# Attention and mixture of experts on one core: weight splits, a table's steps, slots and gate powers moved in their engines' orders

## The chip, the cores and the metric

One core of one Trainium2 chip runs the whole program. The metric is the device time of one execution in microseconds (us). Of the kernel before there are three runs besides the profiled one.

## The reference

A pre-layernorm block on x of 4 x 1024 x 128 in float32, with two parts:

```python
x = x + attn(layernorm(x))         # scores = (h*w_lhs)(h*w_rhs)^T, softmax, times h; 4 sequences of 1024
x = x + ffn(layernorm(x))          # 4096 tokens, 8 experts, top 2
# ffn:
probs = softmax(xf @ router_w.T)
topk_probs, topk_idx = top_k(probs, 2); topk_probs /= topk_probs.sum(-1)
h   = gelu(xf @ w_fc[e] + b_fc[e])         # 128 -> 512
out = h @ w_proj[e] + b_proj[e]            # 512 -> 128
y   = sum over the two experts of gate * out
```

The output has the shape of x. The reference computes every expert for every token; the kernel computes only the two chosen ones.

## The kernel before, in words

Each of the five engines has one instruction stream, written out by hand; an engine does its instructions strictly in that order, and semaphores hold it where it needs another's result. So where a piece of work stands in an engine's stream decides what it can hold up.

**Attention.** The four sequences are batches b = 0 to 3. TensorE (PE) scores a batch in 16 blocks of 128 x 512, VectorE (DVE) takes row maxima (`row_max`, L1559), PE turns the negated maxima (`turn_negs`, L1211) and adds them to the scores, ScalarE (ACT) takes exponents, and PE multiplies them with the rows (`attend`, L1226). h and q are held as a high part (ACT, `high_parts`, L1002 and L1003) and a low part (DVE, `low_parts`, L1500 and L1507), because three products of short parts stand for one product in float32. Half a batch is a unit u, so `low_parts(2b+3)` is for the second half of the next batch; PE waits for it (`parts_made`) in the middle of the routing matmuls of the next batch (`route`, L1238 and L1239). `keep_hrw` (L1518) takes the routing products on DVE and `row_max(b+1, 1)` to `row_max(b+1, 7)` follow.

**Routing.** For each round of tokens (one batch, or half of batch 2) DVE picks the two experts (`picks`), PE counts ranks (`rank_round`, L1250 and L1256), DVE works out slots (`find_slots`, L1716 to L1739) and GpSimd (POOL) takes a power for the gates (`gate_powers`, L864), which `find_slots` waits for. A second layernorm goes with it: `take_stats2` (L1606), `take_moments2` (L1615), `scale_ln2` on POOL (its power is L817), `make_h2` and `high_h2` on ACT, `split_h2` on DVE (L1637).

**Dispatch.** POOL scatters each 128 tokens twice (for two experts) to their slots in memory: 16 indirect DMAs a batch (`dispatch`, L855). `dispatch_own`, `dispatch_max` and `dispatch_next` pace them by exponents and maxima. Batch 2's 16 stand after the batch loop, with `scale_ln2(6)`, `scale_ln2(7)` and `gate_powers(last)` among them. Batch 3's are done during the expert tiles.

**Weights.** w_fc is scaled and split in eight pieces of 512 columns: ACT makes the high part and scales the piece in place (`split_weights`, L1046 and L1047), POOL takes the difference (`low_part`, L825). When the first five are split, POOL clears their memory and stores empty rows from it (`clear_empty`, `store_empty`). PE waits for all eight before the first expert tile.

**Expert tiles.** 24 full tiles of 256 rows and 23 small ones of 128, in the order k = 0 to 46. Step k on PE turns tile k+2's rows (`turn_slots`, L1396), multiplies tile k up (`up`, L1409 to L1411) and tile k-2 down (`down`, L1430). Step 3 ends with a wait for tile 0's bias on DVE and `rank_round(last)`. DVE at step k adds the bias of tile k-3 (L1950), gates it (L1958) and keeps the row numbers of tile k (`keep_rows`, L1931 to L1943); between these it makes the tables that say which slots a tile takes: `second_table` is for tiles 8 to 15, a generator with one instruction a step (L485 to L623), stepped by `beside(k, n)` from the table `STEPS`. SyncE (SP) loads the tiles' slots (L737). Before tile 8 it waits until all scatters of batches 0 and 2 have landed and the second table is made (`more_dispatched(1)`).

## Time and profile before

| | |
|---|---|
| runs | 302.72, 300.7, 301.04 us; median 301.04 |
| profiled execution | 302.37 us, of which 300.6 us are the span of its instructions |
| busy, share of the span | PE 91%, PE weight load 82%, DVE 77%, ACT 65%, POOL 60% |
| mean granted clock of PE | 0.948 |
| chain that ended last | PE 66%, DVE 21%, DMA 5%, issue 4%, POOL 2% |
| first expert tile up | 153.3 us after the start |

Times in the rows are from the start of the span. The granted clock of PE has two levels here, 1.00 (2.4 GHz) and 0.50 (1.2 GHz). A busy share is an average over stages; what a change is worth is read from the stage that it touches. "Idle before" tells how long an engine had nothing to do and what ended that.

### The profile page before, as it was taken

To read this page: it belongs to the slowest core of one execution; us is meant where nothing else is said; L and a number is where in the kernel's file an instruction comes from. 1 tells how busy PE (TensorE), PEld (TensorE's weight loads), DVE (VectorE), ACT (ScalarE), POOL (GpSimd) and SP (SyncE) were. 2 spreads that over 40 slices of the span, in tenths; PEclk is the share of its full clock that TensorE was granted. 3 is DMA by queue.
4 is the path that set the end of the run, shared out by engine and by line. 5 is a ranking of instruction groups with operands and counts; after the bars stand their busy time and mean duration, and the time that the engine had idled before them with its cause. 6 is when DMAs were issued, how large, how long until landed. Compare 5 with 4: busy or idle time off the path is not lost.

```text
span 300.6 us, 8278 instructions
## 1 busy us (share of the span) xinstructions
PE 273.6 (91%) x2221; PEld 245.3 (82%) x2221; DVE 232.5 (77%) x1002; ACT 194.5 (65%) x425; POOL 181.3 (60%) x247
## 2 busy tenths in 40 slices
PE   7999999999999997999998699999999999999500
PEld 2689998888988987878888599999999999999400
DVE  5888899889878897998989668786565666763736
ACT  2437378896469590555679478677788878988300
POOL 8321036017677782687777657777777777777710
PEclk9989999999999996899999599999999999999955
DMA  5970000000401100011161034123433332212886
GB/s 193 410 312 0 0 3 0 3 0 0 146 27 57 45 19 20 28 47 36 60 165 52 29 100 138 56 74 100 115 88 99 99 99 83 83 56 68 346 283 258
DMA packets 15451, 28.52 MB, mean 95 GB/s; under 512 B 3904, under 2 KB 9920, under 8 KB 15152
## 3 DMA queue, kind: packets, MB, share of 16 engines
q1 hardware_dynamic: 10224, 16.88, 17.2%
q0 software_dynamic: 4608, 10.07, 10.0%
q10 hardware_dynamic: 576, 1.05, 1.0%
q8 instruction: 20, 0.33, 0.5%
q14 instruction: 23, 0.19, 0.2%
HBM read 15.83 MB, written 12.16 MB: 93 GB/s over the span
## 4 chain that ended last, share of the span: by engine, by line
PE 66%; DVE 21%; DMA 5%; issue 4%; POOL 2%; POOLq 0%; DVEq 0%; ACT 0%; SPq 0%
PE av_ps L1430 18%; PE av_ps L1226 15%; PE sc_ps L1409 5%; PE sc_ps L1411 4%; PE sc_ps L1410 4%; DVE neg_piece L1559 4%; PE bank L1396 2%; PE sc_ps L1215 2%; PE bank L1198 2%; PE sc_ps L1201 2%; PE sc_ps L1198 2%; PE sc_ps L1204 2%; PE bank L1204 2%; PE bank L1201 2%; DMA results<-prob,result_row 2%
## 5 line engine op out<-in xcount | busy, mean ns | idle before, releaser
L972 POOL DMA_INDIRECT results<-prob,result_row x71 | 69.7, 982 | 21.8 <-issue 14.9
L1121 ACT ACTIVATE raw_fc<-sc_ps,bfc,scale_down 128x128 f32<-128x128 f32 (+1 forms) x188 | 81.3, 530 | 2.1 <-PE sc_ps L1411 1.9
L855 POOL DMA_INDIRECT slots<-stage,slot x64 | 62.7, 980 | 24.5 <-issue 17.8
L1226 PE MATMUL av_ps<-h_all,prob 128*128 128x137 f32 x512 | 74.3, 289 | 2.6 <-DVE q_lo L1507 1.7
L1430 PE MATMUL av_ps<-raw_proj,raw_fc 128*128 x568 | 73.8, 281 | 0.7 <-DVE h_all L1950 0.7
L1226 PEld LDWEIGHTS av_ps<-h_all,prob 128*128 128x128 f32 x512 | 66.9, 192 | 7.5 <-DVE res L1587 2.8
L1430 PEld LDWEIGHTS av_ps<-raw_proj,raw_fc 128*128 128x128 f32 x568 | 68.3, 195 | 2.1 <-issue 1.6
L1409 PE MATMUL sc_ps<-h_all,wfc_hi 128*128 128x128 f16 (+1 forms) x188 | 43.7, 250 | 0.0
L1411 PE MATMUL sc_ps<-h_all,wfc_lo 128*128 128x128 f16 (+1 forms) x188 | 43.6, 250 | 0.0
L1410 PE MATMUL sc_ps<-h_all,wfc_hi 128*128 128x128 f16 (+1 forms) x188 | 43.6, 250 | 0.0
L1950 DVE TENSOR_TENSOR h_all<-av_ps,bpr 128x256 f32<-128x256 f32 (+1 forms) x47 | 16.9, 359 | 30.8 <-PE sc_ps L1411 27.1
L1113 ACT ACTIVATE h_all<-bank 128x512 f16<-128x512 f16 (+1 forms) x47 | 23.5, 501 | 24.8 <-PE sc_ps L1411 24.8
L1559 DVE TENSOR_REDUCE neg_piece<-bank 128x1 f32<-128x512 f32 x32 | 21.9, 685 | 6.2 <-PE sc_ps L1215 3.8
L1021 ACT ACTIVATE prob<-sc_ps 128x512 f32<-128x512 f32 x32 | 18.3, 598 | 9.8 <-PE sc_ps L1215 9.8
L1011 ACT ACTIVATE again<-bank 128x512 f32<-128x512 f32 x16 | 9.5, 595 | 21.1 <-DVE neg_piece L1559 21.1
L1559 DVE TENSOR_REDUCE neg_piece<-sc_ps 128x1 f32<-128x512 f32 x32 | 21.9, 683 | 1.2 <-PE sc_ps L1204 1.1
L1958 DVE TENSOR_SCALAR prob<-h_all,row_gate 128x128 f32<-128x128 f32 x71 | 19.7, 304 | 1.4
L1409 PEld LDWEIGHTS sc_ps<-h_all,wfc_hi 128*128 x188 | 18.5, 99 | 1.5 <-issue 0.2
L1411 PEld LDWEIGHTS sc_ps<-h_all,wfc_lo 128*128 x188 | 18.6, 99 | 1.3
L1410 PEld LDWEIGHTS sc_ps<-h_all,wfc_hi 128*128 x188 | 18.6, 99 | 1.0
L1396 PE MATMUL bank<-ident,slots_in 128*128 128x128 f16 x142 | 15.6, 222 | 0.1
L1198 PE MATMUL bank<-hT_hi,q_hi 128*128 128x512 f32 x32 | 14.8, 463 | 0.0
(208 smaller groups left out, 533.5 us busy)
## 6 DMA issues: line engine op xcount, KB each, us to landing
slots_in<-slots SPq DMA_DIRECT2D x24, 132.0 KB, 2.5
raw_fc<-in_w_fc_dram SPq DMA_DIRECT2D x1, 2048.0 KB, 11.2
raw_proj<-in_w_proj_dram SPq DMA_DIRECT2D x1, 2048.0 KB, 15.6
res<-in_x_dram SPq DMA_DIRECT2D x3, 512.0 KB, 5.7
slots_in<-slots SPq DMA_DIRECT2D x23, 66.0 KB, 2.2
results<-prob,result_row POOLq DMA_INDIRECT x71, 2.3
slots<-raw_fc POOLq DMA_DIRECT2D x2, 528.0 KB, 4.1
slots<-stage,slot POOLq DMA_INDIRECT x64, 2.4
```

The costliest lines, as they stand in the source:

```text
L855: pool.indirect_dma_start(out=slots[:, :], out_offset=bass.IndirectOffsetOnAxis(ap=slot[:, n, k:k + 1], axis=0), in_=stage[:, b % 2, t, :] ...
L972: pool.indirect_dma_start(out=results[:, :], out_offset=bass.IndirectOffsetOnAxis(ap=result_row[a][:, h:h + 1], axis=0), in_=gated[a][h], ...
L1113: act.activation(xT[:, a % NH, 0:n], bank[a % 2][:, :].bitcast(F16)[:, 0:n], ACT.Copy).then_inc(xT_made, 1)
L1121: ins = act.activation(hid[:, a % NH, c, 0:halves_of(k) * P], up_ps(k, c), ACT.Gelu_apprx_tanh, bias=bfc[:, e, c:c + 1], scale=scale_down[ ...
L1198: pe.matmul(o, q_hi[:, a, rows], hT_hi[:, a, cols], start=True, stop=False, skip_group_check=True)
L1226: mm = pe.matmul(att[:, t, 0:AUG], probT[:, m % RING, t * P:(t + 1) * P], h_aug[:, b % 2, exp_rows(n), :], start=(n % BT == 0 and t % 2 == ...
L1396: mm = pe.transpose(o[:, part * w + h * P:part * w + (h + 1) * P], x, ident16[:, :])
L1409: pe.matmul(o, wfc_hi[:, e, of], xT[:, a % NH, 0:w], start=True, stop=False, skip_group_check=True)
L1410: pe.matmul(o, wfc_hi[:, e, of], xT[:, a % NH, w:2 * w], start=False, stop=False, skip_group_check=True)
L1411: mm = pe.matmul(o, wfc_lo[:, e, of], xT[:, a % NH, 0:w], start=False, stop=True, skip_group_check=True)
L1430: mm = pe.matmul(o, hid[:, a % NH, c, rows], wpr[:, e, c, :], start=(c == 0 and h == 0), stop=(c == HC - 1), skip_group_check=True)
L1559: dve.tensor_reduce(neg_piece[:, r // TU, r % TU, c:c + 1], block_bank(n), AX_X, ALU.max, negate=True).then_inc(max_made, 1)
```

## The change

Six edits, all of order:

1. POOL: `low_part(5)`, `(6)`, `(7)` are made in batch 1 (5 before `clear_empty`, 6 after `store_empty`, 7 behind `scale_ln2(2)` and ahead of batch 0's scatters) instead of batch 2. In batch 2 all five `dispatch_own(1)` scatters come before `scale_ln2(4)`; two did before.
2. ACT: `split_weights(5)`, `(6)` in batch 1 behind `high_h2(1)` and before `high_parts(5)`, `(7)` at the start of batch 2, instead of between batch 2's exponents.
3. PE: two matmuls on constant data (`stay_busy(2)`) in batch 0 after the first five routing tiles.
4. DVE at the end of batch 1: `find_slots(0)` and `add_logits(2)` right behind the last `shift_again`, ahead of `low_parts(5)`; `split_h2(1)` and `take_stats2(2)` behind `keep_hrw(2)`.
5. DVE at the tiles: `second_table` is stepped at tiles 1 to 5 and inside `find_slots(last)`, not at tiles 1 and 2 alone.
6. POOL: `gate_powers(last)` is put ahead of scatter 12 of batch 2, not behind it.

```diff
--- before.py
+++ after.py
@@ -829,6 +829,7 @@
                 pool.wait_ge(inv_made, u + 1)
 
             EMPTY_PIECES = -(-E * H * ROW // HID)
+            assert EMPTY_PIECES + 3 == PIECES
 
             def clear_empty():
                 pool.wait_ge(w_split, EMPTY_PIECES)
@@ -923,16 +924,15 @@
                     gate_powers(ROUNDS_BY[b - 1] - 1)
                 if b == 1:
                     beside_sums(2 * b)
-                    for i in range(3, EMPTY_PIECES):
+                    for i in range(3, EMPTY_PIECES + 1):
                         low_part(i)
                     clear_empty()
                     for half in range(2):
                         store_empty(half)
+                    low_part(EMPTY_PIECES + 1)
                 if b == B - 2:
-                    beside_sums(2 * b)
-                    for i in range(EMPTY_PIECES, PIECES):
-                        low_part(i)
-                    dispatch_own(b - 1, 0)
+                    for part in range(2):
+                        dispatch_own(b - 1, part)
                 if b == 0:
                     pool.wait_ge(peak_made, 1)
                     pool.partition_all_reduce(peaks[:, :], peak[:, :], P, RMAX).then_inc(peaks_made, 1)
@@ -945,9 +945,9 @@
                 if b + 1 < B:
                     scale_ln2(2 * b)
                 if b == 1:
-                    dispatch_own(b - 1, 0)
-                if b >= 1 and b + 1 < B:
-                    dispatch_own(b - 1, 1)
+                    low_part(EMPTY_PIECES + 2)
+                    for part in range(2):
+                        dispatch_own(b - 1, part)
 
             for i in range(8):
                 dispatch(B - 2, i)
@@ -955,10 +955,9 @@
             for i in range(8, 11):
                 dispatch(B - 2, i)
             scale_ln2(2 * B - 1)
-            for i in range(11, 13):
-                dispatch(B - 2, i)
+            dispatch(B - 2, 11)
             gate_powers(len(ROUNDS) - 1)
-            for i in range(13, SCATTERS):
+            for i in range(12, SCATTERS):
                 dispatch(B - 2, i)
 
 
@@ -1057,6 +1056,8 @@
                 if b == 1:
                     split_weights(0)
                     split_weights(1)
+                if b == B - 2:
+                    split_weights(7)
                 keep_again(b, 0)
                 if b == 1:
                     split_weights(2)
@@ -1081,13 +1082,13 @@
                         normalise(2 * b + 2 + u, t + 1)
                     if n in (3, 5) and b == 1:
                         split_weights((n + 3) // 2)
-                    if n in (3, 5, 7) and b == B - 2:
-                        split_weights((n + 7) // 2)
                     if n >= BT - 2 and b >= 1 and b != B - 2:
                         for t in (0, 1) if n == BT - 2 else (2, 3):
                             make_h2(2 * b - 1, t)
                         if n == BT - 1:
                             high_h2(2 * b - 1)
+                            if b == 1:
+                                split_weights(5)
                 keep_rows(2 * b + 1)
                 for n in range(BT, EXPS):
                     if n in (BT + 2, BT + 3) and b == B - 2:
@@ -1097,6 +1098,8 @@
                             high_h2(2 * b - 1)
                     if n == BT + 1 and b + 1 < B:
                         high_parts(2 * b + 2)
+                    if n == BT + 5 and b == 1:
+                        split_weights(6)
                     if n == BT + 5 and b + 1 < B:
                         high_parts(2 * b + 3)
                     exponent(b, n)
@@ -1299,6 +1302,7 @@
                     attend(b - 1, 15)
                 if b == 0:
                     route(0, range(5))
+                    stay_busy(2)
                 pe.wait_ge(again_kept, TU * b + 3)
                 turn_negs(2 * b)
                 pe.wait_ge(again_kept, TU * b + 4)
@@ -1864,12 +1868,10 @@
                     find_slots(ROUNDS_BY[b - 1] - 1, measure)
                     steps(norm, 2)
                 if b + 1 < B:
-                    if b == 1:
-                        split_h2(2 * b - 1)
                     low_parts(2 * b + 2)
                     for r in (2, 3):
                         shift_again(b, r)
-                if b == B - 2:
+                if 1 <= b < B - 1:
                     find_slots(b - 1)
                     add_logits(2 * b)
                 if b == 0:
@@ -1878,20 +1880,18 @@
                     low_parts(2 * b + 3)
                 if b == 0:
                     find_scales()
-                if 1 <= b < B - 2:
-                    find_slots(b - 1)
                 if b + 1 < B:
 
-                    if b != B - 2:
+                    if b == 0:
                         add_logits(2 * b)
                     if b == B - 2:
                         early = picks(ROUNDS_BY[b] - 2)
                         steps(early, 6)
                     row_max(b + 1, 0)
-                    if b != B - 2:
+                    if b == 0:
                         take_stats2(2 * b)
                     keep_hrw(b + 1)
-                    if b == B - 2:
+                    if b >= 1:
                         take_stats2(2 * b)
                         split_h2(2 * b - 1)
                 if b == B - 1:
@@ -1910,7 +1910,7 @@
             choose = picks(last)
 
 
-            STEPS = {0: choose, 1: second_table, 2: second_table, 6: late_table, 7: late_table, 8: late_table, 9: late_table,
+            STEPS = {0: choose, 1: second_table, 2: second_table, 3: second_table, 4: second_table, 5: second_table, 6: late_table, 7: late_table, 8: late_table, 9: late_table,
                      10: small_table, 11: small_table, 12: small_table, 13: small_table}
 
             def beside(k, n=1):
@@ -1986,14 +1986,14 @@
                     add_bias(k - 3, (a - 3) % NB)
                     gate(k - 3, (a - 3) % NB)
                 if k == 4:
-                    find_slots(last)
+                    find_slots(last, lambda: beside(k))
                 for j in range(rows_by(k - 1), rows_by(k)):
                     keep_rows(j, j % NB)
                 if k >= 6:
                     add_bias(k - 3, (a - 3) % NB)
                     beside(k)
                     gate(k - 3, (a - 3) % NB)
-                beside(k, {0: 30, 1: 6, 2: 40, 6: 3, 7: 3, 8: 3, 9: 40, 13: 40}.get(k, 3))
+                beside(k, {0: 30, 1: 3, 2: 0, 3: 2, 4: 8, 5: 40, 6: 3, 7: 3, 8: 3, 9: 40, 13: 40}.get(k, 3))
                 if k == NTILES - 1:
                     add_results(0)
                 if k == 2:
```

## Rows read from the trace of the kernel before

**Rows 1.** Windows: length, busy time of PE, PEld, DVE, ACT, POOL, granted clock, DMA.

```profile
16.00:20.20 4.20, 3.74 (x28) 3.43 (x27) 3.92 (x17) 1.79 (x3) 0.56 (x2) 0.98 0.99 425
20.20:23.60 3.40, 3.40 (x9) 2.64 (x9) 2.66 (x14) 1.88 (x5) 2.27 (x5) 0.52 0.16 63
...
115.80:122.60 6.80, 6.80 (x23) 5.89 (x24) 4.96 (x21) 0.60 (x1) 2.11 (x3) 0.51 0.07 22
...
163.60:167.00 3.40, 1.00 (x9) 0.81 (x8) 3.12 (x23) 3.31 (x7) 1.29 (x2) 0.97 0.13 42
167.00:173.80 6.80, 5.96 (x38) 5.27 (x39) 4.67 (x24) 2.38 (x6) 4.80 (x4) 0.51 0.10 32
```

**Rows 2.** Timeline of DVE and POOL, end of batch 2: start, length, instruction, idle before.

```profile
109.01 3.16 DVE L1716 TENSOR_TENSOR pick<-pick,rank 128x64 f32<-128x64 f32 x2
...
108.56 3.38 POOL L825 TENSOR_TENSOR wfc_lo<-raw_fc,wfc_hi 128x512 f16<-128x512 f32 x3
```

**Rows 3.** Timeline of PE, the wait that follows in batch 3's routing.

```profile
115.16 0.47 PE L1226 MATMUL av_ps<-h_all,prob 128*128 128x137 f32 x2 [1.75 <-DVE q_lo L1507]
```

**Rows 4.** Timeline of PE at steps 3 (its rank round), 5 and 6 of the tiles.

```profile
167.84 0.25 PE L1250 MATMUL av_ps<-taken,before 128*128 128x80 f16 x1 [3.25 <-DVE h_all L1950]
...
174.14 0.39 PE L1396 MATMUL bank<-ident,slots_in 128*128 128x128 f16 x4
...
177.46 0.39 PE L1396 MATMUL bank<-ident,slots_in 128*128 128x128 f16 x4
```

**Rows 5.** Timeline of DVE at steps 1 to 3 of the tiles.

```profile
163.50 0.42 DVE L563 TENSOR_TENSOR chosen<-past,per_expert 128x256 f32<-128x256 f32 x1
...
164.30 0.16 DVE L569 TENSOR_SCALAR of_expert<-of_expert 128x8 f32<-128x8 f32 x1
...
166.95 0.16 DVE L1693 TENSOR_TENSOR step_down<-best 128x8 f32<-128x8 f32 x1
...
167.36 0.42 DVE L1950 TENSOR_TENSOR h_all<-av_ps,bpr 128x256 f32<-128x256 f32 x1
```

**Rows 6.** Timeline of POOL: scatters 12 and 15 of batch 2 and the gates' power.

```profile
164.21 0.98 POOL L855 DMA_INDIRECT slots<-stage,slot  x1 [0.30 <-issue]
167.40 1.67 POOL L864 TENSOR_TENSOR gate<-euler,gap 128x8 f32<-128x8 f32 x1 [2.20 <-DVE gap L1698]
...
172.04 0.96 POOL L855 DMA_INDIRECT slots<-stage,slot  x1 [0.30 <-issue]
```

**Rows 7.** Line L737, SP's loads of tiles: tile 8's issue, and the landings.

```profile
L737 SPq DMA_DIRECT2D slots_in<-slots x1: 333/333/333, 175.1 to 175.1; - x1
...
DMA to landing us min/median/max: 2.3/2.5/2.7
```

**Rows 8.** Timeline of ACT, its first work in batch 2.

```profile
82.33 0.60 ACT L1011 ACTIVATE again<-bank 128x512 f32<-128x512 f32 x1 [4.11 <-DVE neg_piece L1559]
```

**Rows 9.** Timelines of DVE and PE, the edge from batch 1 to 2.

```profile
78.04 0.35 DVE L1716 TENSOR_TENSOR pick<-pick,rank 128x64 f32<-128x64 f32 x2
...
81.62 0.68 DVE L1559 TENSOR_REDUCE neg_piece<-bank 128x1 f32<-128x512 f32 x1
...
80.39 0.25 PE L1239 MATMUL bank<-rw_parts,hT_lo 128*128 128x8 f32 x1
...
87.33 0.60 PE L1211 MATMUL bank<-ident,neg_cols 128*128 128x128 f32 x4
```

**Rows 10.** Timelines of DVE and PE, the edge from batch 2 to 3.

```profile
118.45 0.29 DVE L1518 TENSOR_REDUCE h_all<-bank 128x64 f32<-128x128 f32 x1 [1.68 <-PE bank L1239]
...
120.29 0.68 DVE L1559 TENSOR_REDUCE neg_piece<-bank 128x1 f32<-128x512 f32 x1
...
127.02 0.63 PE L1211 MATMUL bank<-ident,neg_cols 128*128 128x128 f32 x4
```

**Rows 11.** Timelines of POOL and DVE: a small POOL power beside a DVE instruction.

```profile
160.98 1.05 POOL L817 TENSOR_TENSOR rstd<-var,minus_half 128x4 f32<-128x4 f32 x1
...
161.15 0.22 DVE L1679 TENSOR_TENSOR pick<-pick,first_id 128x64 f32<-128x64 f32 x1
```

## The prediction

> **What bounds the kernel now.** I began with the page: PE is busy 91% of the span, so a gain must come from PE's idle time or its clock. PE's waits by line came next and hold only two that matter: 3.25 us at the tiles' rank round and 1.75 us in batch 3's routing. Then the granted clock by windows, because a short wait can cost more than itself. The reader is to see three stretches at half level, 20.2 to 23.6, 115.8 to 122.6 and 167.0 to 173.8; ahead of the third PE was busy 1.00 of 3.40 us [rows 1]. The last two follow the two waits.
>
> The first wait begins on POOL. Its three low parts run from 108.56 to 111.94, and two DVE picks started at 109.01 need 3.16 us [rows 2]. The second half's low q, behind them on DVE, holds PE from 113.41 to 115.16 [rows 3]. The second wait begins on DVE: the second table's steps stand ahead of tile 0's bias, so PE idles from 164.59 to 167.84 [rows 4, 5].
>
> A third limit has no wait yet. POOL's last scatter of batch 2 starts at 172.04 [rows 6], SP's load of tile 8 at 175.1, and a load lands after 2.3 to 2.7 us [rows 7]; PE turns that tile at 177.46 [rows 4]. It is just in time: PE cannot get to step 6 earlier than this chain allows.
>
> **The change part by part.**
>
> Splits on ACT (edit 2). The same six activations are moved. Piece 7 falls into the 4.11 us in which ACT waits at the start of batch 2 [rows 8]. Cost nothing, covered by idle time; if pieces 5 or 6 found none, each would put about 1.3 us before an exponent or high part. Batch 2's exponents lose three splits, but PE paced them; I take no gain.
>
> Low parts (edit 1). POOL has 3.38 us less at 108.56 and as much more earlier: 1.13 a piece. Pieces 5 and 6 delay only scales that are not due. Piece 7 stands ahead of batch 0's scatters, which run back to back, and with a later second-layernorm scale (below) they come about 1.75 us later (1.13 and some 0.6), and so does `gate_powers(1)`, from 108.56 [rows 2] to 110.3. The picks cost 0.35 where no low part runs [rows 9] against 3.16: DVE wins 2.8 us there, and the slots' chain then reaches its wait for the power only at about 110.9 (109.01, the edge's 0.9 below, 1.0 of slots), 0.5 us after it. The three `dispatch_own(1)` scatters put ahead of `scale_ln2(4)` go into time in which POOL waited; by batch 2's scatters about 0.6 us are left of this, and `scale_ln2` has its moments no earlier.
>
> Reorder on DVE (edit 4). `find_slots(0)` fills a DVE gap, but `take_stats2(2)` and `split_h2(1)` now stand between `keep_hrw(2)` and the second row maximum. Routing ends on PE at 80.64, so that maximum can start at 80.68 plus 1.84, the distance from L1518 to L1559 in the same order one batch later [rows 10], 82.52, against 81.62 [rows 9]. It sets `keep_again`, the scores behind it and `turn_negs(4)`: +0.9 us at 87.33. Between +1.0 and 0, if PE has slack that I don't see; I take +0.9, because the rows stand back to back.
>
> The edge to batch 3. PE comes to its wait at 113.41 + 0.9 = 114.31; low q, 2.8 us sooner but for the edge's 0.9 and some 0.3 of wait for ACT's high q, is ready at about 113.6 by PE's wake at 115.16. So the wait goes. PE went from 115.16 to `keep_hrw` at 118.45 [rows 3, 10], 2.65 us of it at half level; at full level that is about 1.97 us, so `keep_hrw` is at 116.3 and the maximum at 118.1. From there DVE is back to back in the rows: 127.02 - 120.29 = 6.73 us [rows 10], whatever PE's clock. `turn_negs(6)` comes at 124.85, so attention ends **2.15 us** earlier, the 0.9 included. Ends: 0.9 later (wait and half level stay) and 3.1 earlier (no edge cost).
>
> Two busy matmuls (edit 3). At half level nine matmuls take 3.40 us, 0.38 each [rows 1], so two take less than that each at full level, and PE is idle 0.46 us of 16.0 to 20.2. They cost 0 to 0.3 us. If they hold the clock, 3.40 us at half level shrink by half, 1.7; DVE then binds part of it, so **-1.6**. Ends 0.3 and -1.7. What speaks for it: only narrow routing products and that idle precede the fall.
>
> The tiles (edits 5 and 6), in times of before. In `keep_rows(2)` L563 starts at 163.50 as now; the way to L569 is 0.80 [rows 5]; one more step and the last two row instructions take about 0.53; then from L1693 to L1950 0.41 as now: tile 0's bias starts at 165.24, not 167.36, and the rank round at 165.72. PE's idle shrinks from 3.25 to 1.13 us. A full tile is 3.32 us (177.46 - 174.14) [rows 4]; rank round and step 4 took 6.30 us at half level, and take some 3.72 at full. So PE is at step 6 at 165.72 + 3.72 + 3.32 = 172.8. The second table's last steps fall into `find_slots(last)`, about 170.2, before anyone needs them; if that cover were gone, tile 8's load would wait for the table.
>
> But tile 8 isn't there. The power starts when the gap is made, at 165.28. From power to last scatter were 4.64 us (172.04 - 167.40) with three scatters behind it; edit 6 makes it four, and one is 0.96 + 0.30 = 1.26 [rows 6]. POOL is free at about 163.3 (0.30 before 164.21, and 0.6 sooner), so the moved scatter, which fitted before the power, is lost to waiting. Last scatter 171.18; load 3.06 later; turned 2.36 after that: 176.6 against 177.46, **-0.86** [rows 4, 6, 7]. PE idles 3.8 us. That is longer than the 3.25 us after which the level fell, so I expect half level again: **+2.6** (6.30 - 3.72), between 0 (level holds, or fell at the 1.13 us idle and ran out under the stall) and 3.4 (6.80 us wholly at half level [rows 1]).
>
> Sum: -2.15 - 1.6 - 0.86 + 2.6 = -2.0. The profiled execution takes 302.37 us, 1.33 above the median of the runs, 301.04; the forecast is 300.4 for the one and **299.0** for the other.
>
> **A rule weighed against a row.** POOL's scales of batch 1 move later by the two pieces, beside DVE instructions with two inputs from SBUF. In the trace a POOL power runs from 160.98 to 162.03 and a DVE instruction of that kind started in it at 161.15 takes 0.22 us [rows 11]: no hold. The Trainium skill (SBUF — State Buffer, Who interferes with whom) says that such a DVE instruction contends with a GpSimd instruction that reads SBUF, and that the later one is fully blocked. The three low parts agree with it, this small power does not; by the rule up to 1.05 us would come on top at batch 2's maxima and the sum would be -1.0, by the row it is -2.0. I take the row, the same operation and shape.
>
> **Rivals.**
> 1. The busy matmuls don't hold the clock: all else as forecast, 301.04 - 0.4 = 300.6. For: 0.45 us of work in 4.2 us is little. Against: routing mixed with `attend` keeps full level in other batches.
> 2. Tile 8's stall costs no clock: 301.04 - 4.6 = 296.4. For: PE may be at half level already and arrive later. Against: 1.13 us amid dense matmuls is less than any wait that a fall follows.
> 3. Slower: `low_part(7)` ahead of batch 0's scatters. If `gate_powers(1)` ends more than 1 us later than worked out (after 113), `find_slots(1)` waits for it, `low_parts(7)` with it, PE's wait and half level at 115 come back with the edge's 0.9, the busy matmuls save little, and the tiles cost 1.7: 0.9 + 1.7 and about 0.5 of added wait, 304.1. Against: 0.5 us margin on DVE and 0.7 on PE.
>
> **How the numbers follow.** Forecast 0.36, rival 1 0.22, rival 2 0.26, rival 3 0.16. About 1% (3.0 us) is what a measurement can tell from no change. Faster by more: rival 2 almost whole and the third of the forecast in which the half level is short, 0.35. Slower by more: half of rival 3 and a little beside, 0.10. Within: 0.55. The range goes from below rival 2 to inside rival 3, 295.8 to 303.3; the forecast's own, with the half level's price 0 to 3.4 reduced to 1.3 to 3.4, is 297.7 to 299.8.
>
> **What would show it.** Right: no half level before the tiles; DVE's L1716 of batch 2 under 0.5 us; PE's L1226 without its 1.75 us; rank round idle near 1.1 us; the gates' power starting right at DVE's gap with POOL idle before it; a PE wait of nearly 4 us at tile 8's turn, half level behind it. Wrong: a half level at 20 or 115; a power idle under 1 us, which makes edit 6 a gain; no stall at step 6, which would mean that the scatters came sooner than POOL's rows allow.

## The result, and the profile after

The changed kernel takes **297.6 us** (median of 4 runs, 297.55 to 297.99), the kernel before in the same comparison 301.11 (300.7 to 302.72). The ratio is 0.9875, with a 95% interval of 0.9839 to 0.9911: 3.5 us faster, where 299.0 was forecast. (The quotient of the two medians is 0.9883.) It is clearly faster than no change, and by its medians it is 1.2%, over the 1% that the prediction took as the least that a measurement can tell; but that 1% lies inside the interval. The forecast of 299.0 was a gain of 0.7%. The profiled execution took 297.55 us, so it stands for its median; that of the kernel before was 1.33 us above its own, so between the two profiled executions there are 4.8 us, not 3.5.

The page of the changed kernel: its span, its busy times, and PE's granted clock in 40 slices of 7.4 us. The last line is the granted clock of the kernel before, in 40 slices of its own span. Here and below, rows that the argument doesn't need are left out between those shown.

```profile
span 295.8 us, 8282 instructions
PE 269.2 (91%) x2223; PEld 240.1 (81%) x2223; DVE 229.1 (77%) x1002; ACT 194.9 (66%) x425; POOL 181.6 (61%) x247
PEclk9999999999999999999999979999999999999955
PEclk9989999999999996899999599999999999999955
```

The span is 4.8 us shorter, and PE is busy for as large a share of it as before. Apart from the last two slices, which are alike in both, only one slice is left below full level. The first three windows of [rows 1], one from the tiles' rank round to step 5, and two at the turn of tile 8 say which (us, then PE's busy time with the number of instructions, granted clock, DMA share, GB/s):

```profile
16.00:20.20 4.20, 4.20 (x30) 1.00 1.02 437
20.20:23.60 3.40, 3.40 (x21) 1.00 0.11 39
115.80:122.60 6.80, 5.97 (x32) 1.00 0.12 41
161.50:169.80 8.30, 7.44 (x73) 1.00 0.13 42
169.80:172.20 2.40, 0.00 (x0) 1.00 0.38 90
172.20:175.70 3.50, 3.46 (x19) 0.58 0.65 176
```

The two stretches at half level in attention are gone, and so is the one after the tiles' rank round. A new one begins at 172.2, behind 2.4 us in which PE did nothing. Of PE's waits by line (us in total, times, longest), these name the cause:

```profile
PE bank L1400 <- DMA slots_in<-slots: 2.4, 1, 2.4
...
PE av_ps L1253 <- DVE h_all L1950: 0.9, 1, 0.9
PE av_ps L1434 <- issue: 0.8, 1, 0.8
```

The 3.25 us at the rank round are 0.9 here, and the 1.75 us for the low q in batch 3's routing have no line any more. In their place PE waits 2.4 us for the rows of tile 8, and 0.8 us in step 4. The timeline of PE gives the checkpoints of attention: `turn_negs(1)`, the second turn of batch 0, and `turn_negs(4)` and `turn_negs(6)`, the first turns of batches 2 and 3 (start, us, engine, line, operation, out<-in):

```profile
33.36 0.60 PE L1214 MATMUL bank<-ident,neg_cols 128*128 128x128 f32 x4
86.57 0.60 PE L1214 MATMUL bank<-ident,neg_cols 128*128 128x128 f32 x4
123.06 0.63 PE L1214 MATMUL bank<-ident,neg_cols 128*128 128x128 f32 x4 [0.41 <-DVE neg_cols L1579]
```

Before, the second and third were at 87.33 and 127.02 [rows 9, 10]. On DVE, the edge from batch 1 to 2 and the picks of batch 2:

```profile
79.01 0.29 DVE L1522 TENSOR_REDUCE h_all<-bank 128x64 f32<-128x128 f32 x1 [1.71 <-PE bank L1242]
80.86 0.68 DVE L1563 TENSOR_REDUCE neg_piece<-bank 128x1 f32<-128x512 f32 x1
108.23 0.36 DVE L1720 TENSOR_TENSOR pick<-pick,rank 128x64 f32<-128x64 f32 x2
109.09 0.16 DVE L1730 TENSOR_SCALAR gate_sum<-gate 128x8 f32<-128x8 f32 x1
111.25 0.74 DVE L1511 SCALAR_TENSOR_TENSOR q_lo<-bank,w_d,q_hi 128x512 fp32r<-128x512 f32 x1
```

The two picks take 0.36 us, against 3.16 beside the low parts [rows 2]. The second half's low q is ready at 111.99; its user on PE, which stood at 115.16 [rows 3], now runs without a wait. POOL, first at `gate_powers(1)` in batch 2, then around the tiles' gates:

```profile
107.23 1.68 POOL L865 TENSOR_TENSOR gate<-euler,gap 128x8 f32<-128x8 f32 x1
158.47 1.08 POOL L856 DMA_INDIRECT slots<-stage,slot  x1 [0.47 <-issue]
161.12 1.67 POOL L865 TENSOR_TENSOR gate<-euler,gap 128x8 f32<-128x8 f32 x1 [1.58 <-DVE gap L1702]
166.88 0.96 POOL L856 DMA_INDIRECT slots<-stage,slot  x1 [0.30 <-issue]
```

`gate_powers(1)` ends at 108.91, 0.35 us later than before. POOL then stands idle 1.58 us ahead of the tiles' power, where a scatter fitted before, and the last scatter of batch 2 starts at 166.88. PE in the first tiles, the rank round, step 4 with its second product, and the turns of the tiles' rows in steps 5, 6 and 7:

```profile
161.57 0.21 PE L1253 MATMUL av_ps<-taken,before 128*128 128x80 f16 x1 [0.85 <-DVE h_all L1950]
164.41 2.05 PE L1434 MATMUL av_ps<-raw_proj,raw_fc 128*128 x16 [0.77 <-issue]
166.29 0.39 PE L1400 MATMUL bank<-ident,slots_in 128*128 128x128 f16 x4
172.22 0.40 PE L1400 MATMUL bank<-ident,slots_in 128*128 128x128 f16 x4 [2.44 <-DMA slots_in<-slots]
177.40 0.39 PE L1400 MATMUL bank<-ident,slots_in 128*128 128x128 f16 x4
```

And SP's queue, whose first load in this window is that of tile 8 (5 loads grouped):

```profile
169.95 5.32 SPq L737 DMA_DIRECT2D slots_in<-slots  x5
```

**Where the time went.** Attention ends 3.96 us sooner (127.02 to 123.06). The rank round comes 6.27 us sooner (167.84 to 161.57), tile 8 is turned 5.24 us sooner (177.46 to 172.22) [rows 4], and step 6 then takes 5.18 us instead of 3.3, because PE runs it at half level. Step 7 began at 180.81 before, so there 180.81 - 177.40 = 3.4 us are left. The remaining 1.4 us between the two spans arise at the very end. Before, DVE waited there for the load of the early results:

```profile
279.80 0.69 DVE L1965 TENSOR_TENSOR res<-res,hT_hi 128x512 f32<-128x512 f32 x1 [0.52 <-DMA hT_hi<-results]
```

Its two additions stood ahead of the last three biases, and PE's last product waited 0.72 us for DVE. In the changed kernel this load is issued 6.2 us sooner (269.97, was 276.13), DVE has no such wait, and the last gates end 4.2 us sooner (279.49, was 283.73). The other 0.6 us arise between these gates and the last addition. It is partly chance that the 3.4 us at step 7 equal the difference of the medians, since the profiled executions differ by 4.8.

### The profile page after: what moved, and what is told of

It is laid out like the page before. It is cut to its first block, busy times and chain, and to the rows that moved or that the text cites. A ratio compares the mean times of both kernels' runs of the same rounds, so it can differ in the third digit from the quotient of the medians.

```text
span 295.8 us, 8282 instructions
## 1 busy us (share of the span) xinstructions
PE 269.2 (91%) x2223; PEld 240.1 (81%) x2223; DVE 229.1 (77%) x1002; ACT 194.9 (66%) x425; POOL 181.6 (61%) x247
## 4 chain that ended last, share of the span: by engine, by line
PE 69%; issue 10%; POOL 9%; DMA 5%; DVE 5%; ACT 1%; SPq 0%; POOLq 0%; DVEq 0%; ACTq 0%
PE av_ps L1434 20%; PE av_ps L1229 15%; POOL slots L856 7%; PE sc_ps L1413 5%; PE sc_ps L1415 5%; PE sc_ps L1414 5%; PE bank L1400 2%; PE bank L1201 2%; PE sc_ps L1218 2%; PE bank L1204 2%; PE sc_ps L1204 2%; PE sc_ps L1207 2%; PE sc_ps L1201 2%; DMA raw_fc<-results 2%; PE bank L1207 2%
## 5 line engine op out<-in xcount | busy, mean ns | idle before, releaser
L971 POOL DMA_INDIRECT results<-prob,result_row x71 | 68.7, 967 | 23.9 <-issue 12.5
L856 POOL DMA_INDIRECT slots<-stage,slot x64 | 63.6, 994 | 24.7 <-issue 16.1
L1229 PE MATMUL av_ps<-h_all,prob 128*128 128x137 f32 x512 | 73.3, 286 | 0.7 <-DVE lg_part L1594 0.4
L1434 PE MATMUL av_ps<-raw_proj,raw_fc 128*128 x568 | 73.0, 279 | 0.8 <-issue 0.8
L1229 PEld LDWEIGHTS av_ps<-h_all,prob 128*128 128x128 f32 x512 | 66.1, 190 | 5.5 <-DVE res L1591 2.7
L1434 PEld LDWEIGHTS av_ps<-raw_proj,raw_fc 128*128 128x128 f32 x568 | 67.6, 193 | 2.2 <-issue 1.5
L1958 DVE TENSOR_SCALAR prob<-h_all,row_gate 128x128 f32<-128x128 f32 x71 | 20.6, 324 | 1.3
```

Source lines behind the costliest of these rows:

```text
L856: pool.indirect_dma_start(out=slots[:, :], out_offset=bass.IndirectOffsetOnAxis(ap=slot[:, n, k:k + 1], axis=0), in_=stage[:, b % 2, t, :] ...
L971: pool.indirect_dma_start(out=results[:, :], out_offset=bass.IndirectOffsetOnAxis(ap=result_row[a][:, h:h + 1], axis=0), in_=gated[a][h], ...
L1229: mm = pe.matmul(att[:, t, 0:AUG], probT[:, m % RING, t * P:(t + 1) * P], h_aug[:, b % 2, exp_rows(n), :], start=(n % BT == 0 and t % 2 == ...
L1434: mm = pe.matmul(o, hid[:, a % NH, c, rows], wpr[:, e, c, :], start=(c == 0 and h == 0), stop=(c == HC - 1), skip_group_check=True)
```

## The experiments

Each run is compared with the kernel before on the same chip. The runs were made in three groups on three chips; the kernel before had medians of 300.67 (e1 to e4), 301.37 (e5 to e8) and 301.2 (e9 to e12). In the second group e5 is the changed kernel itself, in the third e9 is the kernel of e6; e1 to e4 have no such base beside them and are compared by ratio.

**e1, gates' powers where they were (edit 6 undone).**

```diff
-            dispatch(B - 2, 11)
+            for i in range(11, 13):
+                dispatch(B - 2, i)
             gate_powers(len(ROUNDS) - 1)
-            for i in range(12, SCATTERS):
+            for i in range(13, SCATTERS):
```

> The changed kernel (297.6 us) with edit 6 undone: the gates' last power behind scatter 12 again. Theory (edit 6 costs a scatter's time on the way to tile 8): POOL idles 1.58 us before the power and the scatter fits into that, so batch 2's last scatter starts 1.26 us sooner, PE's wait for tile 8 falls from 2.44 to about 1.2 us. If the half level behind it goes too (it costs 5.18 - 3.32 = 1.86 us), 294.5 us, if it stays, 296.3. Rival (the power is what counts, because the slots of batch 3 wait for it): 297.6 or more, and tile 8's wait unchanged.

Measured: 296.27 us (295.88 to 298.3), ratio 0.9868 [0.9832, 0.9904]. The profiled execution is one of two near 298.3; the other four lie between 295.88 and 296.35. Its last scatter and the turn of tile 8:

```profile
165.81 0.96 POOL L856 DMA_INDIRECT slots<-stage,slot  x1 [0.30 <-issue]
172.08 0.40 PE L1401 MATMUL bank<-ident,slots_in 128*128 128x128 f16 x4 [2.08 <-DMA slots_in<-slots]
```

The scatter is 1.07 us sooner, as it should be when POOL's idle time is filled, and SP issued the load at 168.87 instead of 169.95. But PE could use the rows only 3.21 us later, against 2.27 us (172.22 - 169.95), so 0.14 us arrived. Edit 6 does cost POOL a scatter's time; in this trace the load gave almost all of it back. I had expected a wait of about 1.2 us for tile 8; it is 2.08, and half level follows it (0.50 from 173 to 176 us). The profiled execution belongs to the slower ones; the four near 296 were not profiled.

**e2, without the two busy matmuls (edit 3 undone).**

```diff
                     route(0, range(5))
-                    stay_busy(2)
```

> The changed kernel without its two busy matmuls in batch 0 (edit 3 undone). Theory (they hold the clock): half level from about 20 to 23.5 us again, the second turn of maxima 1.5 us later, 299.1 us. Rival (the level fell in the kernel before for another reason, and the two matmuls do nothing): full level there and 297.6 us.

Measured: 297.16 us (296.06 to 298.56), ratio 0.9881 [0.9844, 0.9918]. Two windows of it:

```profile
20.20:23.60 3.40, 3.40 (x21) 2.96 (x21) 3.30 (x15) 2.77 (x7) 2.33 (x5) 1.00 0.15 58
172.20:175.70 3.50, 3.36 (x31) 3.04 (x32) 1.08 (x6) 1.45 (x4) 2.69 (x3) 1.00 0.63 173
```

Full level at 20 us without edit 3, and full level behind a wait of 2.48 us for tile 8. The theory (299.1 us, half level at 20 us) did not come true in this execution. The runs form two groups: 296.06, 296.06 and 296.27 with a mean granted clock of 0.975 to 0.977, and 298.04, 298.22 and 298.56 with 0.969 to 0.971. The profiled execution is one of the faster. So one kernel's executions differ by about 2 us, and the slower have the lower clock. Where the clock falls in the slower ones, at tile 8 or at 20 us, is not shown, since none of them was profiled. My reason for edit 3 found no support.

**e3, `take_stats2(2)` and `split_h2(1)` ahead of `keep_hrw(2)`.**

```diff
                     row_max(b + 1, 0)
-                    if b == 0:
+                    if b <= 1:
                         take_stats2(2 * b)
+                    if b == 1:
+                        split_h2(2 * b - 1)
                     keep_hrw(b + 1)
-                    if b >= 1:
+                    if b == 2:
                         take_stats2(2 * b)
                         split_h2(2 * b - 1)
```

> The changed kernel, but in batch 1 take_stats2(2) and split_h2(1) stand ahead of keep_hrw(2), in the 1.7 us in which DVE waits for the routing matmuls; the rest of edit 4 stays. Theory (these two behind keep_hrw delay the row maxima and cost the edge 0.7 us): the third batch's first turn of maxima comes about 0.7 us sooner against the second batch's end, 296.9 us. Rival (PE sets the edge, or what is won is lost in the wait for tile 8, whose load hangs on POOL): 297.6 us.

Measured: 296.93 us (295.05 to 297.55), ratio 0.9863 [0.9829, 0.9896].

```profile
85.51 0.60 PE L1214 MATMUL bank<-ident,neg_cols 128*128 128x128 f32 x4
```

From the checkpoint before it, at 66.94, that is 18.57 us, against 19.54 (67.03 to 86.57) in the changed kernel: the edge gives back 0.97 us, the two instruction groups now falling into DVE's 1.71 us of waiting for routing. The gain reaches tile 8, turned at 171.37, behind a wait of 2.60 us and with half level behind it. It supports the step of the prediction that priced edit 4's reorder at +0.9. The median shows a part of it at most; the interval can't tell it from none.

**e4, the parts of the weights made where they were (edits 1 and 2 undone, the scatters left).**

```diff
-                    for i in range(3, EMPTY_PIECES + 1):
+                    for i in range(3, EMPTY_PIECES):
                         low_part(i)
...
-                    low_part(EMPTY_PIECES + 1)
                 if b == B - 2:
+                    beside_sums(2 * b)
+                    for i in range(EMPTY_PIECES, PIECES):
+                        low_part(i)
...
-                    low_part(EMPTY_PIECES + 2)
...
+                    if n in (3, 5, 7) and b == B - 2:
+                        split_weights((n + 7) // 2)
...
```

> The changed kernel with edits 1 and 2 undone but for the order of batch 1's own scatters: low parts 5 to 7 and their splits in batch 2 again. Theory (POOL's low parts hold DVE's slot picks): two picks take some 3 us instead of 0.36, PE waits over 1.5 us in batch 3's routing and falls to half level behind it; attention ends 3.2 us later, 300.8 us. Rival (the gain at this edge came from the reorder on DVE or from the scatters): picks under 0.5 us or no half level, and at most 298.5 us.

Measured: 300.62 us (299.82 to 301.45), ratio 0.9995 [0.9957, 1.0033]. DVE's picks of batch 2, PE's wait in batch 3's routing (total, times, longest), and PE at the rank round and at tile 8:

```profile
108.32 3.17 DVE L1717 TENSOR_TENSOR pick<-pick,rank 128x64 f32<-128x64 f32 x2
```

```profile
PE av_ps L1226 <- DVE q_lo L1508: 1.8, 1, 1.8
```

```profile
163.50 0.21 PE L1250 MATMUL av_ps<-taken,before 128*128 128x80 f16 x1 [1.18 <-DVE h_all L1947]
174.16 0.40 PE L1397 MATMUL bank<-ident,slots_in 128*128 128x128 f16 x4 [2.45 <-DMA slots_in<-slots]
```

The held picks and the 1.8 us are back, and tile 8 is turned 1.94 us later than in the changed kernel. Nearly the whole gain of the change goes with edits 1 and 2 (the interval leaves about 1 us either way). The run undoes both together; the held picks stand beside POOL's low parts, which are of edit 1, and neither edit was undone alone. The trace alone accounts for 1.9 of the 3 us: in this execution (299.82 us) the level did not fall behind the 1.8 us. Two of the four runs, at 301.3 and 301.45, have a mean granted clock of 0.959, against 0.971 in the profiled one. That they are executions in which it fell there is likely, not shown.

**e5, the changed kernel again**, as the base of its group.

> The changed kernel itself, timed again beside the next three, to know how its executions scatter on this chip. Theory (whether an idle stretch of PE is followed by half level differs from execution to execution): its times fall into groups about 1.7 us apart, as those of the runs without the busy matmuls did (296.1 and 298.2), and the upper one goes with the lower mean clock; median 296 to 298. Rival (half level follows tile 8's wait each time): one group at 297.6.

Measured: 298.09 us (296.67 to 299.07), ratio 0.9875 [0.9832, 0.9918], the same ratio; tile 8 again with a wait of 2.46 us and half level behind it. The profiled execution, at 299.07, is the slowest. One run lies apart at 296.67 with a mean clock of 0.976, the other five at 297.72 to 299.07 with 0.970 to 0.972. So executions of the changed kernel itself differ too, but only one of six was of the faster kind, and the median is 0.1 us above what I had expected at most.

**e6, PE kept at work ahead of tile 8's rows.**

```diff
             def turn_slots(k, a):
-                pe.wait_ge(xs_in[a], 16 * (k // NB + 1))
                 if k >= 2:
                     pe.wait_ge(xT_made, k - 1)
+                if k == NB:
+                    for _ in range(9):
+                        pe.matmul(bank[a % 2][:, :], busy[:, 0:P], busy[:, :], start=True, stop=True, skip_group_check=True)
+                pe.wait_ge(xs_in[a], 16 * (k // NB + 1))
```

> The changed kernel with nine busy matmuls of 512 columns, into the free bank, right before PE waits for tile 8's rows. Theory (the wait of 2.4 us itself is set by POOL and the load, and the half level behind it costs 1.86 us on top): the wait shrinks by the 1.95 us that the matmuls take, tile 8 is turned at the same time, no half level follows, step 6 takes 3.3 us and the kernel 1.8 us less than the slower executions of the changed one: about 295.8 us, with all times within 0.5 us of each other. Rival (the half level behind the wait is not worth its price, because later work waits for others anyway): the same median as the changed kernel beside it.

Measured: 296.19 us (295.99 to 296.76), ratio 0.9824 [0.9783, 0.9866].

```profile
169.61 2.10 PE L1396 MATMUL bank<-busy 128*128 128x512 f16 x9
172.26 0.40 PE L1403 MATMUL bank<-ident,slots_in 128*128 128x128 f16 x4 [0.55 <-DMA slots_in<-slots]
175.78 0.39 PE L1403 MATMUL bank<-ident,slots_in 128*128 128x128 f16 x4
```

Tile 8 is turned when it was, 172.26 against 172.21 in e5, but step 6 takes 3.52 us instead of 5.15, and the median is 1.9 us lower. That isolates the price of the half level: 1.6 to 1.9 us. The spread of the six runs shrinks to 0.8 us, from 2.4 in e5. That the matmuls hold the clock, and not chance, rests on all traces together: of the seven without them (the changed kernel, e1 to e5, e7), with waits of 2.08 to 2.67 us for tile 8, five have half level behind the wait; of the six with them (e6, e8 to e12) none has.

**e7, the second table where it was (edit 5 undone).**

```diff
-            STEPS = {0: choose, 1: second_table, 2: second_table, 3: second_table, 4: second_table, 5: second_table, 6: ...
+            STEPS = {0: choose, 1: second_table, 2: second_table, 6: ...
...
-                    find_slots(last, lambda: beside(k))
+                    find_slots(last)
...
-                beside(k, {0: 30, 1: 3, 2: 0, 3: 2, 4: 8, 5: 40, 6: 3, ...
+                beside(k, {0: 30, 1: 6, 2: 40, 6: 3, ...
```

> The changed kernel with edit 5 undone: the second table again stepped at tiles 1 and 2 alone. Theory (tile 8's load bounds step 6 whatever PE does before): the rank round comes 2.1 us later and waits 3 us, the gates' power 2.1 us later too, with edit 6's scatter behind it, so tile 8 is turned 2.1 us later and the kernel takes 2.1 us more, within 1.5 us for where half levels fall. Rival (the idle time only moves from the rank round to tile 8): less than 0.5 us more.

Measured: 300.55 us (298.68 to 302.26, 10 runs), ratio 0.9964 [0.9928, 0.9999], 2.5 us above e5.

```profile
163.76 0.25 PE L1253 MATMUL av_ps<-taken,before 128*128 128x80 f16 x1 [3.33 <-DVE h_all L1950]
174.79 0.40 PE L1400 MATMUL bank<-ident,slots_in 128*128 128x128 f16 x4 [2.67 <-DMA slots_in<-slots]
178.30 0.39 PE L1400 MATMUL bank<-ident,slots_in 128*128 128x128 f16 x4
```

The full wait at the rank round returns, and since the gates' power hangs on the same DVE work (it starts at 163.32 instead of 161.12), tile 8 is 2.58 us late as well. In this execution half level followed the wait at the rank round (163.6 to 167.0 us at 0.56) but not tile 8's wait (step 6 is 3.51 us), while others of the ten took up to 3 us more.

**e8, what the findings point to:** edit 6 undone, `take_stats2(2)` and the splits of batches 1 and 2 ahead of `keep_hrw`, the tiles' ranks ahead of DVE's split, and eight busy matmuls ahead of tile 8. Its edits that are as in e1 and e6 are left out here.

```diff
                     row_max(b + 1, 0)
-                    if b == 0:
+                    if b <= 1:
                         take_stats2(2 * b)
+                    if b >= 1:
+                        split_h2(2 * b - 1)
                     keep_hrw(b + 1)
-                    if b >= 1:
+                    if b == 2:
                         take_stats2(2 * b)
-                        split_h2(2 * b - 1)
...
-                    split_h2(2 * B - 2)
                     keep_ranks(last)
+                    split_h2(2 * B - 2)
```

> The changed kernel with what the runs so far point to: the gates' last power behind scatter 12 again; take_stats2(2), split_h2(1) and split_h2(3) ahead of keep_hrw; keep_ranks(last) ahead of split_h2(6), because PE waits for it 0.8 us in step 4; and eight busy matmuls before the wait for tile 8. Theory (these add): 0.7 to 1.0 us from the edge of batch 1, 0.4 from that of batch 2, 0.5 to 1.1 from the scatter, 1.8 from the clock, about 294.0 us. Rival (all of them end in the wait for tile 8, which the load sets): 295.5 us or more.

Measured: **295.25 us** (294.68 to 296.35), ratio **0.9804** [0.9761, 0.9846], 2.8 us under e5 and 0.9 under e6. The theory was 294.0, its rival 295.5 or more; it lies between.

```profile
162.20 2.05 PE L1438 MATMUL av_ps<-raw_proj,raw_fc 128*128 x16 [0.17 <-issue]
169.42 0.40 PE L1404 MATMUL bank<-ident,slots_in 128*128 128x128 f16 x4
172.94 0.39 PE L1404 MATMUL bank<-ident,slots_in 128*128 128x128 f16 x4
272.22 0.69 DVE L1970 TENSOR_TENSOR res<-res,hT_hi 128x512 f32<-128x512 f32 x1 [1.06 <-DMA hT_hi<-results]
```

Step 4's wait is 0.17 instead of 0.77 us, tile 8 has none, and step 7 begins 2.84 us ahead of e6 (175.78). The span is only 1.5 us shorter than e6's: half of the lead is lost behind step 7. Most of that is lost at the end, where DVE waits 1.06 us for the early results: their load is issued at 268.26, no sooner than in e6 (268.32), and the last gates end only 1.8 us ahead of e6 (276.14, was 277.93). The chain behind this load is the next limit.

**e9 to e12** take the kernel of e6 as their base, since the runs of e6 scattered least.

> The changed kernel with the nine busy matmuls before tile 8's rows, as once before, now as the base of the next three on one chip, because its times lie close together (296.0 to 296.8 before). Theory: 296.2 us and a spread under 1 us again, no half level before the kernel's last stretch.

e9, the base: 296.38 us (295.71 to 297.14), ratio 0.9832 [0.9807, 0.9857]. The spread is 1.4 us, where under 1 was expected: no half level before the end in its trace, but its runs lie no closer together than those of its variants (0.8 to 1.8).

> The base without edit 3's two busy matmuls in batch 0. Theory (they hold the clock in some executions): about half of the executions have half level after the routing and take 1.5 us more, the rest is as the base, so the median is 0 to 1.5 us above the base and the spread 1.5 us or more. Rival (they do nothing): the base's median within 0.3 us and its spread.

e10, edit 3 undone as in e2: 296.63 us (296.11 to 297.86), ratio 0.9855 [0.9828, 0.9882]. The window at 20 us:

```profile
20.20:23.60 3.40, 3.40 (x22) 3.00 (x21) 3.30 (x14) 2.87 (x7) 2.25 (x5) 1.00 0.08 29
```

A second trace at full level without the two matmuls. If they hold anything, it is in some executions only, and the medians allow a few tenths.

> The base with edit 6 undone (the gates' power behind scatter 12). Theory (edit 6 costs a scatter's time on the way to tile 8): tile 8's load is issued 1.1 us sooner; its rows are turned 0.1 to 1.1 us sooner, as the load's landing allows (in the profile of the same step without the matmuls it took 3.1 us and not 2.2), 295.2 to 296.0 us. Rival (the load's landing takes up what the scatter gives): the base's median within 0.2 us.

e11, edit 6 undone as in e1: 296.48 us (296.2 to 297.04), ratio 0.9844 [0.982, 0.9869].

```profile
171.68 0.40 PE L1404 MATMUL bank<-ident,slots_in 128*128 128x128 f16 x4
```

The load is issued 1.3 us sooner (168.64 against 169.9 in e9) and tile 8 is turned 0.56 us sooner, without a wait: here the nine busy matmuls, which end just ahead of it, set the time. The median shows nothing of it. So edit 6 costs between 0.1 and 0.6 us at tile 8 and nothing measurable in the whole.

> The base with edit 4 undone: DVE's order at the end of batch 1 as in the kernel before, while POOL's low parts stay moved. Theory (edit 4 costs the edge 0.7 us but keeps split_h2(1) away from POOL's low parts): split_h2(1) takes over 1.5 us instead of 0.68, because it starts beside them, the low parts of h and q behind it come later, PE waits up to 0.8 us for them, and the sum is within 0.3 us of the base. Rival (nothing meets there, edit 4 only costs): 0.7 us below the base.

e12, edit 4 undone (`split_h2(1)` ahead of `low_parts(4)`, `find_slots(0)` behind `find_scales`, the moments ahead of `keep_hrw(2)`): 296.37 us (296.07 to 297.55), ratio 0.9846 [0.9821, 0.9872], equal to e9. DVE, POOL and PE in batch 1:

```profile
71.09 1.67 DVE L1644 TENSOR_TENSOR stage<-h,stage 128x512 f16<-128x512 f32 x1
```

```profile
68.80 3.40 POOL L825 TENSOR_TENSOR wfc_lo<-raw_fc,wfc_hi 128x512 f16<-128x512 f32 x3 [0.56 <-DVE inv_sum L1590]
```

```profile
86.86 0.60 PE L1214 MATMUL bank<-ident,neg_cols 128*128 128x128 f32 x4
```

With the low parts in their new place, the split that stood at 71.09 would run beside them and take 1.67 us, where it takes 0.67 in e9. `turn_negs(4)` is at 86.86 against 86.47 in e9. So edit 4 costs 0.7 us against the kernel before and saves 0.4 against the old order with edit 1 in place.

## Why the prediction was right, and where its sizes were off

**The edge to batch 3 (edits 1 and 2): right.** Attention was to end 2.15 + 1.6 = 3.75 us sooner and ended 3.96 sooner. The steps hold one by one: picks 0.36 us, no wait for the low q at L1229, full level from 115.8 to 122.6, and DVE back to back from there. The forecast times, less the 1.6 us of edit 3, are also the measured ones: low q 112.0 and 111.99, `keep_hrw` 114.7 and 114.50, the second maximum 116.5 and 116.34. e4 shows the cause by its return. `gate_powers(1)` was to end at 110.3, that is 108.7 less these 1.6 us, and ended at 108.91. Rival 3 needed an end more than 1 us later than worked out; it was 0.2 later.

**The reorder (edit 4): right.** The distance from `keep_hrw(2)` to the second maximum is 80.86 - 79.01 = 1.85 us, 1.84 forecast. From `turn_negs` at 67.03 to 86.57 are 19.54 us, 18.82 before (68.51 to 87.33): +0.7 for +0.9. e3 takes it away again.

**Batch 0's half level (edit 3): the size right, the reason not shown.** `turn_negs(1)` came 1.47 us sooner (34.83 to 33.36), for 1.6 forecast. But e2 and e10 have the same full level and the same checkpoint (33.35 and 33.25) without the two matmuls. The level at 20 us differs between executions. The 1.6 us were a fair term against the profiled execution before, and I booked them to the wrong edit. All traces together say a little more: of the three without the two matmuls (the kernel before, e2, e10) one has half level at 20 us, of the eleven with them none. That fits matmuls that hold the clock as well as a fall that is rare anyway. It stays open.

**The rank round (edit 5): right.** PE's idle time shrank to 0.85 us, 1.13 forecast, with no half level behind it. e7 shows what it is worth: 2.5 us. The runs of e4 and e7 also show that the edits don't add up. Without edits 1 and 2 the rest gives nothing measurable, without edit 5 the rest gives 0.8 to 1.1 us, together they give 3.5. The trace of e7 says a part of why: attention ends 4.0 us sooner than before, as in the changed kernel, but DVE makes the gap and the rank round late, tile 8 hangs on the gap, and it is turned only 2.7 us sooner (174.79, was 177.46). The rest of the loss in e7's median this trace doesn't show.

**Tile 8 (edits 5 and 6): mechanism right, size off by 0.6 us.** Forecast was a PE idle of 3.8 us; it is 2.44. I put the turn at 176.6 - 3.75 = 172.85, and it was at 172.22. The chain agrees link by link: the power starts at 161.12 (161.53 forecast), from there to the last scatter are 5.76 us (5.90), to the load 3.07 (3.06), to the turn 2.27 (2.36). PE for its part was to arrive at 169.05 and arrived at 169.78, because step 4 holds a wait of 0.77 us that I had left out. DVE's ranks, for which it waits, stand behind a split; e8, with the ranks first, has 0.17 us there. That the half level of before had hidden the wait is my reading, not tested. This is my omission: when an engine gets faster, every row that was just in time for it must be looked at again.

**The half level behind the stall: the step that was mis-sized.** I took the 2.6 us that I had derived from the longer stretch before (rank round and step 4, 6.30 us against 3.72). Step 6 took 5.18 us against 3.32 at full level: 1.86. e6 measures it by itself at 1.6 us in the trace and 1.9 in the median. The sum with measured terms is -3.96 at attention's end, -5.24 at tile 8, +1.86 in step 6: -3.4. With mine it was -2.0 (-3.75, -4.61, +2.6). Half of the 1.4 us between them is this term (0.74), the other the sooner tile (0.63).

**What was luck.** The sum was worked out on the profiled execution of before, for which it gave 302.37 - 2.0 = 300.4; the profiled execution after took 297.55. That is off by 2.85 us: the 1.4 above, and 1.4 at the end of the kernel, for which the prediction had no term. Taken from the median, the same sum gave 299.0, off by 1.4. The execution profiled before was a slow one: its mean clock of 0.948 is lower than that of all but one of the 39 runs of the same kernel beside the experiments (0.946 to 0.976), and its three stretches at half level need not all be in a median one. So the forecast for the median took off terms that the median may hold only in part, the 1.6 of edit 3 above all, and had no term for the 1.4 at the end; the two errors pull against each other. The measured 297.6 lies 0.1 us under the range that the prediction gave for its own case (297.7 to 299.8), and a gain over 1%, with a chance of 0.35, came in place of one within it, with 0.55.

**The rivals.** Rival 2, no clock lost behind the stall, 296.4 us, is what some executions seem to do: e2's profiled one, at 296.27, has full level there, and one run in six of e5 took 296.67. It isn't what the typical run of the changed kernel does. I had treated it as one of two fixed outcomes; it is likely one of two outcomes of the same kernel. Rival 1 would have needed half level at 20 us, and rival 3 a late gates' power; neither appears in the profile.

**The rule weighed against a row.** The trace of the changed kernel shows batch 1's second-layernorm scale beside DVE (lines of POOL and DVE in order of start):

```profile
79.28 1.02 POOL L803 TENSOR_TENSOR rstd<-var_eps,minus_half 128x4 f32<-128x4 f32 x1
79.34 0.23 DVE L1527 TENSOR_TENSOR x_logits<-h_all,spread 128x64 f32<-128x64 f32 x1
80.26 0.67 DVE L1641 TENSOR_TENSOR stage<-h,stage 128x512 f16<-128x512 f32 x1
80.38 0.61 POOL L806 TENSOR_TENSOR shift<-neg_mean,rstd 128x4 f32<-128x4 f32 x1
```

A DVE instruction started inside the power takes 0.23 us and is not held, as the row had said. The other way round, POOL's shift, 0.20 us before, takes 0.61 when it starts inside DVE's split and ends 0.06 us behind it. The Trainium skill (SBUF — State Buffer, Who interferes with whom) states that DVE and GpSimd share one pair of ports as an exclusive lock, that the issue order decides who blocks, and, of DVE's two-port modes, that whoever issues first keeps the pair for the whole instruction and the other is fully blocked. POOL's low parts against DVE (0.67 to 1.67 us in e12, 0.36 to 3.17 in e4) and DVE's split against POOL agree with it, POOL's power on 4 columns does not. No cost of it appears in the trace, as the row's value of nothing said.

## What to carry to other kernels

Price a move by what the moved instruction runs beside, not by its own duration: three low parts of 3.4 us in all cost 3 us of the kernel, because two picks and a low q stood in their shadow. When a wait is taken out, follow the next chain in absolute times, from the releaser to the user, and look again at each row that was just in time. Where one wait can't be removed, giving the idle engine empty matmuls to do removed the loss of clock behind it here, worth 1.6 to 1.9 us. And a forecast for the median should start from an execution near the median.

## What the runs showed that was not expected

- **The length of the wait alone does not say whether the clock falls.** Behind waits of 2.08 (e1), 2.44 and 2.46 us (changed kernel, e5) the next step ran at half level, behind 2.48 and 2.67 us (e2, e7) at full level. The runs of e2 alone lie 2 us apart, so it likely differs from execution to execution. The kernel before, with two long waits, spread over 4.2 us in 17 runs; with PE kept busy, the runs of one kernel spread over 0.8 to 1.8 us (e6, e8 to e12, five or six runs each).
- **A load issued sooner did not land sooner.** Tile 8's rows were usable 2.27 us after the issue at 169.95 and 3.21 us after the issue at 168.87 (e1). In e8, issued at 167.05, they were there within 2.37 us. What holds it in e1 was not found.
- **A wait on DVE's side reached DMA.** Undoing the table's order (e7) delays a load by 2.6 us through DVE's gap, POOL's power and four scatters. The table itself, for which SP waits too, doesn't hold that load: its last instruction starts at 162.78 in e7 and at 166.26 in the changed kernel, in both before the last of these scatters starts (169.25 and 166.88).
